# VectorE's order within a step of hop 0, in a three-hop graph kernel

## What is computed

```python
h = relu(layernorm(x)); agg = h; out = 0
for _ in range(3):
    head, tail = agg[src], agg[dst]      # 25,000 rows each
    rel = edge_emb[edge_type]
    att = sum((head @ q_w) * tanh(rel * tail @ k_w), axis=1)
    w   = softmax of att over the edges with equal head
    agg = segment_sum(w * rel * tail) / max(count, 1), then each row over its norm
    out = out + agg + h
return x + out
```

## Time and profile before

| | |
|---|---|
| median of 3 runs | 2251.78 us (2236.15 to 2257.71) |
| the profiled execution | 2228.32 us, its span 2226.2 us |
| busy, share of the span | TensorE 48%, DVE 59%, ACT 36%, POOL 55% |
| first gather of hop 0 | 247 us after the start |
| last Relu of a unit in hop 0 | 922 us after the start |

### The profile page before, as it was taken

The page is one execution under the profiler, slowest core; times in us unless marked ns, Lnnn a source line. Parts: engine busy times, 40 slices in busy tenths (PEclk is TensorE's granted clock), DMA queues, the critical chain, the costliest instruction groups (busy, mean ns, idle before and its releaser), DMA issues. The chain is left out here.

```text
span 2226.2 us, 22847 instructions
## 1 busy us (share of the span) xinstructions
PE 1074.8 (48%) x5076; PEld 876.2 (39%) x5076; DVE 1316.6 (59%) x5932; ACT 802.1 (36%) x2503; POOL 1219.3 (55%) x1218
## 2 busy tenths in 40 slices
PE   0010133333359554675421666878545469777420
PEld 0000122222248443465320445768534348577320
DVE  8888675555653445635841654383756453688970
ACT  0000055555733454523631431271643222524420
POOL 1000455555655666763777777620037676567776
PEclk9999986666655766655555886785767677855555
DMA  8800344444432323313542764530269897657771
GB/s 228 237 8 0 133 142 161 163 154 159 144 97 84 94 87 100 118 64 104 177 156 87 220 196 127 141 124 34 83 166 193 148 181 145 166 159 205 212 207 35
DMA packets 194443, 302.78 MB, mean 136 GB/s; under 512 B 31284, under 2 KB 113536, under 8 KB 189652
## 3 DMA queue, kind: packets, MB, share of 16 engines
q1 hardware_dynamic: 154460, 202.55, 28.0%
q0 software_dynamic: 38400, 72.99, 16.0%
q10 hardware_dynamic: 1448, 25.80, 4.2%
HBM read 175.78 MB, written 130.86 MB: 138 GB/s over the span
## 5 line engine op out<-in xcount | busy, mean ns | idle before, releaser
L550 POOL DMA_INDIRECT tr<-in_x_dram,tidx x200 | 193.8, 969 | 425.7 <-DVEq L778 236.2
L1322 PE MATMUL ps<-rt,wr 128*125 128x128 f32 x1200 | 264.9, 395 | 262.2 <-DVE wr L935 153.3
L1259 PE MATMUL ps<-ident,rt 128*128 128x128 f32 x600 | 129.3, 354 | 456.3 <-DVE rt L997 429.9
L1322 PEld LDWEIGHTS ps<-rt,wr 128*125 128x125 f32 x1200 | 235.2, 293 | 285.3 <-DVE wr L935 171.5
L550 POOL DMA_INDIRECT tr<-agg_d,tidx x200 | 198.6, 993 | 256.1 <-issue 236.8
L1148 ACT ACTIVATE sqj<-ps,invc 125x128 bf16<-125x128 f32 x600 | 213.7, 380 | 289.7 <-PE ps L1322 289.7
L1259 PEld LDWEIGHTS ps<-ident,rt 128*128 128x128 f32 x600 | 88.9, 182 | 483.1 <-DVE rt L997 451.1
L1107 ACT COPY rtT<-ps 128x512 f32<-128x512 f32 x150 | 87.8, 586 | 489.5 <-PE ps L1259 489.5
L562 POOL DMA_INDIRECT ntab_d<-rt,lidx x200 | 209.8, 1049 | 95.7 <-issue 59.3
L562 POOL DMA_INDIRECT out_dram<-rt,lidx x200 | 211.5, 1057 | 89.2 <-issue 60.3
L550 POOL DMA_INDIRECT tr<-ntab_d,tidx x200 | 197.2, 986 | 67.6 <-issue 59.4
(11 more groups left out here) (222 smaller groups left out, 2228.7 us busy)
## 6 DMA issues: line engine op xcount, KB each, us to landing
agg_d<-rt SPq DMA_DIRECT2D x100, 258.0 KB, 2.4
xr<-agg_d SPq DMA_DIRECT2D x100, 258.0 KB, 3.8
relr<-rel_d SPq DMA_DIRECT2D x100, 256.0 KB, 4.2
ntab_d<-rt ACTq DMA_DIRECT2D x15, 1679.7 KB
rt<-in_x_dram SPq DMA_DIRECT2D x13, 1024.0 KB, 6.6
out_dram<-rt SPq DMA_DIRECT2D x13, 1024.0 KB, 4.0
acc_d<-xr SPq DMA_DIRECT2D x50, 258.0 KB, 2.9
rel_d<-relr SPq DMA_DIRECT2D x50, 256.0 KB, 2.3
```

The costliest lines, as they stand in the source:

```text
L550: G.indirect_dma_start(out=row, out_offset=None, in_=table[:, :], in_offset=bass.IndirectOffsetOnAxis(ap=idx[:, n:n + 1], axis=0)).then_in ...
L1259: ins = T.transpose(ps[B_TR][:, t, :], rt[:, g * GT + t, 0:D], ident[:, :])
L1322: ins = T.matmul(ps[B_T + j % 2][0:R, t, :], wr[:, (j % 2) * GT + t, 0:R], rt[:, j * GT + t, 0:D], start=True, stop=True)
```

## The change

Only the order of DVE's program within a step of hop 0 changes. Before, a step began with the new unit's statistics, then those of the chunk, and then the chain, into which the scores, the old unit's products, the new unit's types, the old unit's base rows and the early output were put. After it, a step does in this order: wait for `s_lh`, products of the old unit, base rows of the old unit, types of the new unit, statistics of the chunk, statistics of the new unit, the chain with the scores alone in it, the early output. No instruction is added or taken away, and no other engine's program changes.

```diff
                         older = UNITS[s - 2] if s > 1 else []
+                        if old:
+                            dve.wait_ge(s_lh, s)
+                        for g in old:
+                            product(0, g)
+                        for g in old:
+                            base_rows(g)
+                        for g in unit:
+                            types_hot(g)
+                        if s < NDE:
+                            dve.wait_ge(s_xe[s % XE], 16 * (s // XE + 1))
+                            for t in range(DE):
+                                ch.note(V.bn_stats(stats[:, 4 * GT + t, :], xe[s % XE][:, t, :]))
                         for i, g in enumerate(unit):
                             dve.wait_ge(s_t[g % TS], t_value(0, g))
...
-                        if s < NDE:
-                            dve.wait_ge(s_xe[s % XE], 16 * (s // XE + 1))
-                            for t in range(DE):
-                                ch.note(V.bn_stats(stats[:, 4 * GT + t, :], xe[s % XE][:, t, :]))
                         ch.join()
                         between = []
                         for g in older:
                             between += scores(0, g)
-                        if old:
-                            between += [lambda: dve.wait_ge(s_lh, s)]
-                        between += [lambda g=g: product(0, g) for g in old]
-                        between += [lambda g=g: types_hot(g) for g in unit]
-                        between += [lambda g=g: base_rows(g) for g in old]
-                        if 0 < s <= NDE:
-                            between += [lambda: early_out(s - 1)]
                         if unit:
                             layer_norm(stats, lns[s % 2], 4 * GT + (DE if s < NDE else 0), s_ln, between)
...
+                        if 0 < s <= NDE:
+                            early_out(s - 1)
```

## The result

| | us, median (lowest to highest) | profiled execution | its span |
|---|---|---|---|
| before | 2251.8 (2233.1 to 2257.7), 5 runs | 2228.3 | 2226.2 |
| after | 2189.8 (2178.1 to 2193.9), 5 runs | 2178.1 | 2176.1 |

The time is 0.974 of that before (95% interval 0.971 to 0.977): 58 us less, 51 to 66. The medians are 62.0 us apart. The forecast was 52 less, 2200 us, with a range of 2180 to 2228. The two profiled executions differ by 50.2 us. The size was right. Two of its terms were not, and they missed in opposite directions. The loop that I had described for the kernel before was also not the one that held it.

What follows compares the result with a forecast made beforehand. Bound taken: hop 0's loop of gathers, statistics, chain, product, TensorE and ACT in turn, 27.29 us a step. Savings 41 + 1.5 + 9.6 = 52 us, 2251.8 - 52 = 2200 us; range 2180 to 2228.

Steps and rivals of the forecast that it cites:

- steps 2 to 11: Hop 0's ten early steps: each falls from 27.3 to 23.2 us, saving 41 us, bounds 35 to 52.
- steps 12 to 20: Hop 0's later steps: next to nothing gained, 0 to 3 us, taken as 1.5, since ACT and TensorE set the step.
- The loop of before: Unchanged hop 0 step of 27.29 us: gathers landed, statistics, chain, product, TensorE and ACT in turn.
- The slow stretch: ACT's first copy to next Relu with TensorE's clock low: 11.40 us instead of 9.44, making the step 23.8.
- `back` waiting for the scores: TensorE's `back` of the old unit waits for scores now behind the statistics; next Relu at 22.1 not 21.9, costing 0.2 us.
- POOL keeps up: POOL's gathers in the changed step: 12 us of slack, bound only by issue time, 20.0 us, or 22.7 with longer gathers.
- Two blocked gathers: POOL gathers lengthened beside DVE instructions with two SBUF operands: 2.7 us a step, costing nothing under 23.2.
- Steps 21 and 23: Late hop 0 steps where DVE's norms wait for ACT: product directly behind the scaling, 4.8 us each, 9.6 together.
- Passed on whole: Behind hop 0: nothing takes the gain back, so all 52 us reach the end.
- POOL as the bound: Rival, chance 0.17: gathers lose all two-SBUF-operand DVE time, early hop 0 steps take 25.0 us, total about 2221.
- Idle time only moved: Rival, chance 0.14: product comes early only to wait for ACT and scores; 11 us gained, 2241.
- The store stuck in SP's queue: Rival, chance 0.06: base rows' store waits behind SP's chunk load; at 35 us landing, step 30.4, time 2283, slower.

Runs made afterwards that it cites:

- second profile of before: The unchanged kernel before, run once more for another profile on one of the first two chips: profiled execution 2240.3 us, against 2228.3 in its first.

## Why the prediction was right, and where it was not

- **Total.** 52 us forecast, 58 measured (51 to 66), 50.2 between the two profiled executions; 2200 us forecast, 2189.8 measured. That it came so near is in part luck: steps 2 to 11 gave 8 us too little, steps 12 to 20 gave 10 too much.
- **The loop of before.** I read "gathers, statistics, chain, product, TensorE and ACT in turn". TensorE and ACT were not in it. It closes through the base rows, their store and POOL's eight gathers. With the product alone at the head the step is 25.7 and not nearly 24, because the next two bounds, types and base rows, stand directly behind. No number came out wrong from this, since the step before was measured as a whole and the step after was built up anew from R. But the sum would not have priced a half change rightly.
- **Steps 2 to 11: 41 us forecast, 33 measured between units 1 and 11, 35 at unit 11.** The ends of the term were 35 and 52. The 12.4 us to the first copy were right (12.32). The slow stretch is there in every step (11.6, and the forecast for it was 11.4), while I took a step partly fast, 23.2. With a step of 23.96 on average the term lies just outside its ends, as even the slow one had 23.8. TensorE's first transpose standing 5 us ahead of the others, which I had noted, is what does it: with that gap filled, the step is 21.8.
- **`back` waiting for the scores, 0.2 us.** It costs nothing in after, where TensorE is late by its clock. It does bind once the clock is up.
- **POOL keeps up.** Right: 1.95 us of idle time a step are left. Two blocked gathers are 0.37 and 1.96 us too long in the step shown, 2.3 together (the second from 1.05 to 1.96 over the steps); the forecast was 2.7.
- **Steps 12 to 20: 1.5 us forecast, about 12 measured.** This step failed. It held for units 11 to 18 (1.0). From unit 18 on I said that TensorE's own work hides the product. It hid it all but 0.3 to 2.3 us, and such a gap could cost more than itself: behind it the transposes and what follows ran partly at the lower clock. The steps from unit 18 to 21 gave 3.8, 4.4 and 2.4 us (gaps of 1.91, 1.25 and 0.33, and 1.6, 3.2 and 1.5 in the stretches behind them).
- **Steps 21 and 23: 9.6 us forecast, 7.8 measured** (2.7 and 5.1; the rest, 22 and 24, even out). Against the second profile of before it is 10.6 (2.4 and 8.2).
- **Passed on whole.** 54.8 us at unit 25, 55.7 at hop 1, 50.1 at the end. Hop 1 was 4.0 us longer and hop 2 0.6. Over the ten profiles of the first two chips and of before and after, hop 1 goes from 442.6 to 454.6 us and hop 2 from 294.1 to 325.2, so neither is shown to be the change's doing.
- **The rivals.** POOL as the bound did not come about, and the steps are under 25.0; it is one of the bounds at 21.8. Idle time only moved: no. The slow clock in all ten steps, its first condition, was met, but the later steps gave back more than that took. The store stuck in SP's queue: POOL's wait for it became shorter, not longer.

## What to carry over

Before an instruction is moved, follow the loop that holds the step from wait to wait until it comes back to its own start, one step later. At each handover the next engine must have stood idle until the piece before it ended; where it had time to spare, that path is not the loop. Here the five pieces through the base rows pass this, and the path through TensorE and ACT had 5 us to spare. A forecast step length that comes out doesn't yet name the loop: with the products alone moved, two loops lay 0.4 us apart. Where another engine's work stands between bursts of TensorE's, the price of a gap need not be its length: read the same instruction's duration behind a gap and without one, and count the burst at that duration. Moving one half of a change (base rows without the product) can be worse than nothing, since a wait that moves to the head delays all that stayed behind it.

## What was not expected of the hardware

- Without a gap between TensorE's sums and its transposes the stretch behind them took 7.81 us ahead of units 19 to 21. Behind gaps of 0.33 to 2.28 us in the kernel before it took 9.3 to 11.8, but 7.81 behind one of 0.68. 14 fill matmuls on constants, in 4.9 us of idle time, raised the granted clock of the loop from 0.61 to 0.79 and took 2.1 us off each step. By the Trainium skill (TensorE: Matmul & The Clock Gate, "What's actually happening") the clock is set by how busy the engine has been recently. The fill's results are used by nothing, and the run agrees.
- An indirect gather beside a two-operand DVE instruction of 2.28 us took 1.9 to 3.0 us instead of 0.94. Cut in four pieces, 2.49 us in all, it delayed the gather by only 0.36.
- Hop 2, with the same code and data, took 294 to 325 us in different executions.
- One chip ran the kernel before in 2619 us where the two others took 2255 and 2257.
